# Decoder layer on one core: norm chains on VectorE at the start, unread products ahead of the first tokens, values a slot later, late turning

## The reference

```python
x = x + attn(layernorm(x))            # 32 heads of 32, 8 key/value heads, rotary, causal
x = x + xattn(layernorm(x), context)  # a matmul of two fake-quantised operands
x = x + ffn(layernorm(x))

def attn(x):
    q, k, v = split(x @ w_qkv.T + b_qkv)          # 1024, 256, 256 wide
    q, k = apply_rope(q), apply_rope(k)           # pairs (even, odd) turned by cos and sin
    scores = where(causal, q @ k.T / sqrt(32), -1e20)
    return softmax(scores) @ v @ w_o.T + b_o
def xattn(x1, x2):                                # x2: the context, 1024 x 1024
    fake_quant = lambda x, s, z: (clip(round(x / s + z), 0, 255) - z) * s
    return fake_quant(x1) @ fake_quant(x2)
def ffn(x):
    base = x @ W_org.T
    q = x.mean(axis=tokens) @ Wq.T                # one query of 128 per batch
    coeffs = softmax(q @ lora_keys.T / sqrt(128)) # 8 experts
    h = x @ lora_down                             # 8 experts of 64: 512 wide
    return base + (coeffs * h) @ lora_up
```

## Time and profile before

| | us |
|---|---|
| median of 3 runs | 791.65 |
| lowest, highest | 790.46, 792.01 |
| the profiled execution | 793.04 |
| its span (first to last instruction) | 791.2 |
| TensorE busy in it | 693.7 (88%) |
| TensorE's weight loads (beside its matmuls) | 556.9 (70%) |
| VectorE busy | 421.7 (53%) |
| ScalarE busy | 429.9 (54%) |
| GpSimd busy | 307.6 (39%) |

### The profile page before, as it was taken

One profiled execution on the slowest core, in us unless ns is written; L12 is line 12 of the kernel. 1 busy time (PEld: TensorE's weight loads), 2 busy tenths in 40 slices (PEclk: granted clock), 3 DMA queues, 4 the chain that ended last, 5 costly groups with the idle time before them and its releaser, 6 DMA issues.

```text
span 791.2 us, 12919 instructions
## 1 busy us (share of the span) xinstructions
PE 693.7 (88%) x4608; PEld 556.9 (70%) x4608; DVE 421.7 (53%) x1123; ACT 429.9 (54%) x1025; POOL 307.6 (39%) x384
## 2 busy tenths in 40 slices
PE   3999599999999899998768687799996787799998
PEld 3897477788777677875546475588875666588886
DVE  3366377776777536656648353433336569831212
ACT  3325378878787667797665653646314660512320
POOL 5337655543342534471304710505713011525510
PEclk9998899999999999999979698999999797699999
DMA  7504856563445606225350430403425342323102
GB/s 251 193 2 159 245 174 170 157 172 97 136 121 177 201 23 189 64 75 163 112 164 1 130 75 4 120 14 108 160 88 179 100 148 85 120 93 107 41 13 94
DMA packets 43823, 93.49 MB, mean 118 GB/s; under 512 B 5488, under 2 KB 5872, under 8 KB 42224
## 3 DMA queue, kind: packets, MB, share of 16 engines
q1 hardware_dynamic: 40176, 76.94, 30.2%
q0 software_dynamic: 3584, 15.73, 8.3%
HBM read 72.72 MB, written 19.92 MB: 117 GB/s over the span
## 4 chain that ended last, share of the span: by engine, by line
PE 58%; DVE 15%; POOL 9%; ACT 8%; issue 6%; DMA 2%; SPq 1%; DVEq 0%; ACTq 0%
PE dense L1023 37%; PE probt L917 7%; PE score L905 5%; PE pv L932 4%; POOL w_lo L1558 3%; PE score L1023 2%; DVE stats L1295 2%; DVE prob_all L1251 2%; ACT stage L1060 2%; ACT prob_all L1104 2%; POOL ln_s L828 2%; DVE act_t L1318 1%; POOL prob_all L1575 1%; POOL ln_s L830 1%; DVE prob_all L1344 1%
## 5 line engine op out<-in xcount | busy, mean ns | idle before, releaser
L1023 PE MATMUL dense<-w_hi,act_t 128*128 128x512 f32 (+1 forms) x684 | 233.4, 404 | 23.6 <-DVE act_t L1318 10.7
L1251 DVE CUSTOM_DVE_ANT_0 prob_all<-score,mask_sb 128x128 f32<-128x128 f32 (+3 forms) x256 | 123.7, 487 | 141.4 <-PE score L905 139.5
L1558 POOL TENSOR_TENSOR w_lo<-stage,w_hi 128x512 fp32r<-128x512 f32 x89 | 116.4, 1316 | 191.5 <-ACT w_hi L1064 191.2
L1104 ACT ACTIVATE prob_all<-prob_all,neg_max 128x128 f32<-128x128 f32 (+3 forms) x256 | 143.2, 559 | 72.4 <-DVE neg_max L1251 70.6
L1023 PEld LDWEIGHTS dense<-w_hi,act_t 128*128 128x128 f32 x684 | 133.3, 200 | 51.8 <-DVE act_t L1318 11.8
L1023 PE MATMUL dense<-w_lo,act_t 128*128 128x512 f32 (+1 forms) x372 | 138.5, 393 | 5.6 <-DVE xres L1389 3.1
L1023 PE MATMUL dense<-act_t,w_hi 128*128 128x512 f32 x408 | 139.6, 424 | 1.8 <-DVE xres L1367 1.8
L917 PE MATMUL probt<-ident_sb,prob_all 128*128 128x128 f32 x640 | 113.9, 277 | 1.4 <-ACT prob_all L1113 1.1
L905 PE MATMUL score<-k_stack,q_stack 96*128 96x128 f32 (+3 forms) x256 | 92.1, 364 | 13.9 <-DVE neg_max L1251 7.5
L1064 ACT ACTIVATE w_hi<-stage 128x512 fp32r<-128x512 f32 x117 | 71.9, 624 | 50.9 <-PE dense L1023 31.1
L1113 ACT ACTIVATE prob_all<-probt 128x128 f32<-128x128 f32 (+3 forms) x160 | 68.2, 426 | 47.0 <-PE probt L917 46.0
(11 more groups left out here) (156 smaller groups left out, 916.0 us busy)
## 6 DMA issues: line engine op xcount, KB each, us to landing
q_stack<-rope_dram POOLq DMA_DIRECT2D x16, 768.0 KB, 7.4
stage<-in_w_qk SPq DMA_DIRECT2D x40, 256.0 KB, 3.0
rope_dram<-act_t SPq DMA_DIRECT2D x40, 256.0 KB, 3.3
stage<-in_w_o SPq DMA_DIRECT2D x32, 256.0 KB, 3.0
stage<-in_ctx_kv SPq DMA_DIRECT2D x24, 256.0 KB, 3.1
stage<-in_w_org SPq DMA_DIRECT2D x24, 256.0 KB, 2.8
xres<-in_x SPq DMA_DIRECT2D x8, 512.0 KB, 6.6
prob_all<-in_x SPq DMA_DIRECT2D x8, 512.0 KB, 6.8
```

The lines of the kernel that those rows point to most:

```text
L1023: last = engine.matmul(dst, lhs, rhs, start=(k == 0 and c == 0), stop=(k == g.kts - 1 and c == len(pairs) - 1))
L1104: engine.activation(prob[:, u % P_SLOTS, 0:length], prob[:, u % P_SLOTS, 0:length], ACT.Exp, bias=neg_max[:, m:m + 1], scale=-1.0, accum_o ...
L1251: engine.tensor_tensor_reduce(prob[:, u % P_SLOTS, 0:length], score_bank[u % 2][:, 0:length], mask_sb[:, S - length:S], -1.0, HIGHEST, ALU ...
L1558: engine.tensor_tensor(slot_lo(p, 0, NW), raw_of(p), slot_hi(p, 0, NW).bitcast(F32), ALU.subtract).then_inc(g_piece, 1)
```

## The change

It has these parts:

- **Start.** The norm chains of norm (1, 0) run on VectorE. VectorE zeroes a 128x512 buffer (`blank`, the space of a query stack not yet in use), and TensorE runs sixteen 128x512 products on it into a bank of PSUM that nobody reads before its own first product overwrites it (`keep_clock`). The tokens of the next tile are turned in the middle of a tile's steps. SyncE fetches the last two x tiles behind the weight pieces, and ScalarE and VectorE have another order of their first steps to go with it.
- **Units.** The product with the values, and all that hangs on it, stands one unit later (`PV_LAG` 5; output products are ready one slot later too). A context piece is rounded one slot after its input was made, where the slot holds a unit. On VectorE the row maximum and the copies of turned probabilities stand ahead of the low parts of tokens. The odd pieces of the first base product of batch 0 have their low part on VectorE.
- **Behind the units.** A tile is turned only when its source lies 5.0 planned microseconds back instead of 1.2 (`LATE_TURN_US`), and quantising stands at the head of a slot on VectorE instead of its end.

The diff, cut to its core:

```diff
 PROBT_SLOTS = 6
+PV_LAG = 5
+BLANKS = 16
+LATE_TURN_US = 5.0
+TOKENS_LAG = 1
 MAX_SLOTS = 8
...
 TERMS = 3
-CHAINS_ON_VECTOR = ((2, 1), (3, 1))
+CHAINS_ON_VECTOR = ((1, 0), (2, 1), (3, 1))
 EARLY_LAGS = 2.0, 3.5, 4.5, 6.0, 9.5
...
             if cross:
-                self.note("round", j, p)
+                self.note("round", j + 1 if unit else j, p)
             else:
...
             return p % 2 == 0
-        return p < 8 and p % 2 == 1 or piece["kind"] == "q" and piece["b"] == 0 and piece["nb"] < 4 or piece["kind"] == "out" and p % 2 == 1
+        return p < 8 and p % 2 == 1 or piece["kind"] == "q" and piece["b"] == 0 and piece["nb"] < 4 or piece["kind"] == "out" and p % 2 == 1 or piece["kind"] == "base" and piece["b"] == 0 and piece["nb"] == 0 and p % 2 == 1
...
                 source = ("third", b, t) if which == 2 else ("apply", which, b, t)
-                if not self.past(j, source, 3 if unit else 1, now, 1.2):
+                if not self.past(j, source, 3 if unit else 1, now, 1.2 if unit else LATE_TURN_US):
                     continue
...
                     self.note("turn", j, (which, b, t, half))
-                    self.note("tokens", j + 1 if unit else j, (which, b, t, half))
+                    self.note("tokens", j + TOKENS_LAG if unit else j, (which, b, t, half))
                     halves.append(j)
...
             last = self.first_unit_slot + NT * GROUP * (NKV * g.b + k + 1) - 1
-            return j >= last + 9
+            return j >= last + PV_LAG + 5
         if g.kind == "cross":
...
         w_spaces += [(k_stack[:, 0, :], k_stack[:, 1, :])]
+        blank = q_stack[:, 0, 0, :]
         spare = values_sb[:, :, :, :].rearrange("p b t c -> p (b t c)")
...
         v_const = sem("v_const")
+        v_blank = sem("v_blank")
         v_round = sem("v_round")
...
             fetch(1)
+            fetch(2)
             load_x(0, 1)
-            fetch(2)
             fetch(3)
-            load_x(0, 2)
             engine.dma_start(bias_v[:, :], b_v.to_broadcast([P, VW])).then_inc(d_bv, 16)
...
             fetch(5)
-            load_x(0, 3)
             fetch(6)
             fetch(7)
+            load_x(0, 2)
+            load_x(0, 3)
             engine.dma_start(bias_qk[:, :], b_qk).then_inc(d_bqk, 16)
...
+            def keep_clock():
+                e.wait_ge(v_blank, 1)
+                for _ in range(BLANKS):
+                    engine.matmul(dense_bank[0][:, :], blank[:, 0:P], blank, start=True, stop=True)
...
                 u = j - first_unit
-                if j < NT:
+                if j == 0:
+                    keep_clock()
                     for half in range(2):
-                        turn_tokens(1, 0, j, half)
+                        turn_tokens(1, 0, 0, half)
                 for halves in at["turn"].get(j, ()):
...
                 for s in range(first, end):
+                    if j < NT - 1 and s == first + plan.token_steps // 2:
+                        for half in range(2):
+                            turn_tokens(1, 0, j + 1, half)
                     if plan.steps[s][0].kind == "down" and plan.steps[s][1:] == (0, WEIGH_AT):
...
                     step(s)
-                if 0 <= u - 4 < UNITS and (u - 4) % GROUP == GROUP - 1:
-                    values((u - 4) // GROUP)
-                for gi in ends_at(u, 4):
+                if 0 <= u - PV_LAG < UNITS and (u - PV_LAG) % GROUP == GROUP - 1:
+                    values((u - PV_LAG) // GROUP)
+                for gi in ends_at(u, PV_LAG):
                     turn_inverse(gi)
...
-            for made in range(4):
+            for made in range(2):
                 make_high(made)
             normalise(1, 0, 0)
+            make_high(2)
             for half in range(2):
                 tokens_high(1, 0, 0, half)
-            for made in range(4, 8):
+            make_high(3)
+            for made in (4, 5):
+                make_high(made)
+            normalise(1, 0, 1)
+            for made in (6, 7):
                 make_high(made)
...
                 if j < NT - 1:
-                    normalise(1, 0, j + 1)
+                    if j:
+                        normalise(1, 0, j + 1)
                     for half in range(2):
                         tokens_high(1, 0, j + 1, half)
-                for gi in ends_at(u, 5):
+                for gi in ends_at(u, PV_LAG + 1):
                     take_out_inverse(gi)
...
                     spread(gi)
-                for gi in ends_at(u, 7):
+                for gi in ends_at(u, PV_LAG + 3):
                     attn_high(gi)
...
+            engine.memset(blank[:, :].bitcast(F32), 0.0).then_inc(v_blank, 1)
             engine.memset(ones_r[:, :].bitcast(F32), 1.0).then_inc(v_const, 1)
-            for t in range(2):
-                for part in range(2):
-                    norm_stats(1, 0, t, part)
-            for made in (1, 3):
-                low_piece(made)
+            for part in range(2):
+                norm_stats(1, 0, 0, part)
+            low_piece(1)
             for half in range(2):
                 tokens_low(1, 0, 0, half)
+            low_piece(3)
+            for part in range(2):
+                norm_stats(1, 0, 1, part)
             for made in (5, 7):
...
                 u = j - first_unit
+                if j < NT - 1:
+                    for half in range(2):
+                        tokens_low(1, 0, j + 1, half)
                 if j < NT - 2:
...
                         norm_stats(1, 0, j + 2, part)
-                if j < NT - 1:
-                    for half in range(2):
-                        tokens_low(1, 0, j + 1, half)
                 if j == NT + 2:
...
                     constants()
+                if 0 <= u < UNITS:
+                    maximum(u)
+                if 0 <= u - 3 < UNITS and probt_on[u - 3] == "vector":
+                    take_out_turned(u - 3)
+                if not 0 <= u < UNITS:
+                    for b, t in at["second"].get(j, ()):
+                        quantise_second(b, t)
                 for which, b, t, half in at["tokens"].get(j, ()):
...
                         route_mean(b)
-                if 0 <= u < UNITS:
-                    maximum(u)
-                if 0 <= u - 3 < UNITS and probt_on[u - 3] == "vector":
-                    take_out_turned(u - 3)
                 for m, part in rotate_at.get(j, ()):
...
                     invert(gi)
-                for gi in ends_at(u, 6):
+                for gi in ends_at(u, PV_LAG + 2):
                     scale_values(gi)
...
                     norm_stats(*half)
-                for b, t in at["second"].get(j, ()):
-                    quantise_second(b, t)
+                if 0 <= u < UNITS:
+                    for b, t in at["second"].get(j, ()):
+                        quantise_second(b, t)
                 for b, t in at["third"].get(j - 1, ()):
...
                     load_stacks(gi)
-                for gi in ends_at(u, 7):
+                for gi in ends_at(u, PV_LAG + 3):
                     attn_low(gi)
...
                     add_output_bias(0, bias_at[j])
```

## The result

| | us |
|---|---|
| before, median of 4 (lowest, highest) | 791.83 (790.46, 793.52) |
| changed, median of 4 (lowest, highest) | 755.16 (754.24, 760.09) |
| changed / before | 0.9549, 95% interval 0.9502 to 0.9595 |
| the changed kernel in a second comparison (`again`) | 758.33, 0.9564 (0.9537 to 0.9591) |
| its profiled execution, span | 754.4, 752.6 |

The change made the kernel 34.5 to 35.7 us faster. The forecast was 768.0 with a range of 757 to 782: the direction was right, the size was a third too small.

A forecast was written before the change was run, and what follows sets the result against it. The prediction took TensorE's work plus four idle holes as the bound. Its gains, 8.9 + 1.5 + 6 + 7.5 = 23.9 us, taken from the profiled 793.04 gave 769.1, so 768 at the median, range 757 to 782.

The forecast's parts named there:

- start: Program start up to the first score: chains on VectorE and earlier tiles bring it 8.9 us earlier, bounds 4.2 and 11.1.
- values and out later: Units, 97 to 345: values and out products a slot later cut TensorE's waits, 1.5 us gain, bounds -1 and 3.5.
- rounding later: Units, 345 to 428: rounding a slot later removes VectorE's 23.0 us of waiting, 8 us gain, a third of it.
- odd base pieces on VectorE: Units: four low parts of the first base product move to VectorE beside its idle time, worth nothing.
- maximum first: Units, 428 to 543: tokens' low parts stand behind the row maximum eight times, 2 us loss.
- late turning: Behind the units: out steps ahead of the transposes fill their waits, 7.5 us gain, bounds 2 and 10.
- Rival 2: Units and tail: if the row maximum paces slots, the middle opens and the gain is 33.4, so 758; chance 0.2.
- The 3.2 us of the unread products: Program start: unread products raise the clock, so the first tile's transposes and 24 products save 3.2 us; bounds 0 and 3.2.
- Rival 3: Program start: the clock falls between unread products and transposes; the start loses 1 to 3 us, 771; chance 0.07.
- the collision that I allowed for: Program start: VectorE's chain and GpSimd's low parts share ports, 1.1 us per collision, one or two per chain.
- It is a move, priced 0: Units to behind the last unit: eight dense steps at 0.67 us, 5.3 us, only change place, at no cost.
- Rival 4: Units, 428 to 543: token parts behind the maximum make it slower, 796 at 3.5 us per group; chance 0.04.

The follow-up runs named there:

- before_round_later: Kernel before with context pieces rounded one slot after their input as the only change: 777.88 us, 0.9834.
- no_round_later: Changed kernel with context pieces rounded in the slot of their input again: 765.08 us, 0.9676.
- no_late_turning: Changed kernel with turning behind the units at 1.2 planned us and quantising at the end of VectorE's slot, as before: 763.37 us, 0.9653.
- gap_filled: Changed kernel with eight more unread 128x512 products between the first key products and the second tile's transposes: 753.78 us, 0.9529.
- no_unread_products: Changed kernel without the sixteen unread products: 754.45 us, 0.9529.
- start_and_late: Changed kernel without any of its edits in the units, so start and late turning only: 772.62 us, 0.9766.
- before_round_low: Kernel before with both the rounding a slot later and the odd low parts of the first base product on VectorE: 769.45 us, 0.9728.
- values_lag_4: Changed kernel with values and out products a slot earlier again (PV_LAG 4): 756.09 us, 0.9565.
- same_and_late_sum: Changed kernel with maximum behind tokens' low parts, no unread products, and context sum behind units 5.0 planned us after its last piece, not 0.6: 754.29 us, 0.9525.
- start_only: Changed kernel with its edits in the units and late turning undone, so only the start is left: 785.38 us, 0.9925.
- more_low_parts: Changed kernel with eight more unread products in the start's gap, maximum behind tokens' low parts, second base product's odd pieces also on VectorE: 755.81 us, 0.9544.

## Why the prediction was too small

By the steps of its sum, forecast against measured:

| step | forecast | measured |
|---|---|---|
| start | 8.9 | 5.9 alone |
| values and out later | 1.5 | 0 (by removal: 5.4 in the units, -5.1 behind them) |
| rounding later | 8 | 13.1 alone, 8.9 by removal |
| odd base pieces on VectorE | 0 | 6.4 alone, 5.1 by removal |
| maximum first | -2 | -3.9, -0.6 and -0.8 in three pairs |
| late turning | 7.5 | 12.6 with the start, 7.0 to 8.2 by removal |

The two halves measured on the kernel before (start with late turning 18.5, rounding with low parts 21.5) come to 40.0, the whole to 34.5 to 35.7; some 5 us are lost between them, little more than the noise of such a sum (3 to 4 us).

**The step that failed first** is "Odd base pieces move to VectorE, four low parts beside idle time: nothing". I looked at what the move costs VectorE and never at what it frees on GpSimd. In the waits of TensorE from 428 to 543, of which the earlier trace rows show one line, the line above it is the longer one:

```profile
PE dense L1023 <- POOL w_lo L1558: 7.6, 5, 3.5
```

And the chain of waits of the kernel before shows it between 432 and 456, in rows that I had not read:

```profile
432.50 0.26 POOL ln_s L833
432.77 1.73 POOL w_lo L1558
434.59 0.21 POOL ln_s L821
...
438.16 2.47 POOL w_lo L1558 x2
440.63 0.53 POOL k_stack L1535
...
445.38 1.23 POOL w_lo L1558
446.65 1.65 PE dense L1023 x3
...
451.35 1.27 POOL w_lo L1558
452.62 1.26 POOL act_t L1569
453.87 1.23 POOL w_lo L1558
455.15 0.97 PE dense L1023 x3
```

GpSimd has norm chains, six low parts (7.9 us) and the issue of two loads (`k_stack`, `q_stack`) one behind the other, and TensorE's base products hang on its last low part. Its busy share is small in the table (41.32 of 115), which is why I passed it over; but for some 20 us it was the engine in series. With the odd low parts on VectorE as the only change (`before_low_parts`) GpSimd's low parts are 4.5% of the chain of waits from 424 to 452, where they were 22.0% of it from 424 to 460, and the whole is 6.4 us faster. TensorE's own waits for them fall only from 7.6 to 6.2 us, and those for VectorE's low parts of tokens from 7.1 to 4.7. The step that failed is thus a cost put at nothing on the engine that the work left.

**The second** is "I take 8 us, a third of the VectorE wait": the rounding is worth 13.1 alone. The mechanism held: with this edit alone VectorE's waits for ScalarE's context input fall from 23.0 to 10.3 us, and TensorE's scores wait less for the maximum. Here are these waits of TensorE over all units, in the kernel before and in `before_round_later`:

```profile
PE score L905 <- DVE neg_max L1251: 7.5, 9, 1.7
```

```profile
PE score L905 <- DVE neg_max L1251: 2.8, 5, 1.1
```

That is 4.7 us; the rest of the gain isn't put down to one wait. The stretches from score 160 to 192, 192 to 224 and 224 to the last go from 73.6, 81.8 and 74.5 to 67.6, 71.6 and 69.7 us, with two steps fewer in each (1.3 us), and the mean granted clock in them from 0.98, 0.85 and 0.93 to 1.00, 0.90 and 1.00. The bound that I gave for rounding and maximum together, +13, held the rounding alone; to the sum I brought 8. Rival 2, the middle opens, was the nearer case (758 forecast). Its condition, that the row maximum paces the slots, is borne out only in part, by these 4.7 us.

**The start** came near the forecast at the first score of the first profiled execution (10.3 against 8.9), and that was luck of the execution: it was 4.0 in `again`, and the start alone gives 5.9. The 3.2 us of the unread products are not there. What is late next was in my own text ("TensorE is there at 15.9", "ready 17.8"); I counted this wait as 1.9 us and did not ask what the clock does in it. Rival 3 had the clock fall between the unread products and the transposes. That happened in two of the nine profiled executions (`no_round_later`, `no_late_turning`), in three more it fell in the first tile, and in these five tile 3 ended earliest; in the other four it fell behind the 1.8 us of waiting.

The rule on the shared ports (the Trainium skill, SBUF — State Buffer, "Who interferes with whom") is borne out in part. GpSimd's steps beside VectorE's low parts still stretch (0.66 for a step of 0.34), but VectorE's chain ran at its full pace, 2.58 us, though a low part of GpSimd (1.29 us) ran beside its first half: the collision that I allowed for didn't come. And transposes do run at the higher clock, 1.06 us for eight, as the row had it; by the Trainium skill (TensorE: Matmul & The Clock Gate, "Part 4: PE-mode transpose") they shouldn't. In the same place of the program eight of them took 1.06 us in `gap_filled` and 1.94 in `no_unread_products`. The measurement decides.

**Moved steps priced at nothing.** "It is a move, priced 0" is too cheap. With late turning, 324 steps behind the last unit take 245.4 us and 316 take 234.0 (the changed kernel and `start_and_late`); without it 254.5 and 245.2 (`no_late_turning` and the kernel before). Eight steps cost 11.4 and 9.3 us there, not 5.3. They are not alike: the six that move with the rounding cost 4.4 us on the kernel before (249.6 against 245.2), near the 4.0 of their price, and the two that move with the lag cost 5.1 more, with late turning (245.4 against 240.3) as without (254.5 against 249.4 in `before_round_low`). So what was priced wrong is the lag, whose out products also come a slot later. Part of the 11.4 is seen in the timeline of TensorE in the changed kernel, a wait for a low part of GpSimd:

```profile
522.13 0.74 PE L1035 MATMUL dense<-act_t,w_hi 128*128 128x512 f32 x2 [2.57 <-POOL w_lo L1586]
```

In the profiled execution of `values_lag_4` all waits for GpSimd's low parts behind the last score come to 0.9 us, in the changed kernel to 4.2. Why else the lag costs so much there isn't settled. It is why the lag is worth nothing though the units run faster with it. The 5 us lost between the halves stand in the same place: behind the last score they would give 11.2 - 4.2 = 7.0 us, and the changed kernel gives none (245.4 against 245.2).

**Late turning** held as a mechanism (the transposes' waits 14.0 with it undone, 1.7 with it), and 7.5 lies between its measurements. That it gives more where the eight steps aren't moved fits the paragraph above, but I have not shown how; taking the wait inside the context sum away gains nothing, as `same_and_late_sum` shows.

**The maximum** costs something between 0.6 and 3.9 us, and the 2 us that I gave it lie in the middle. The pair with 3.9 has the two-way start in it; the other two, 0.6 and 0.8, are each within the noise, and in the profiled executions all three have shorter units with the maximum behind the tokens (0.8 to 2.0, 3.0 and 4.3 us). Rival 4 didn't happen: TensorE waits 4.4 us for the tokens' low parts where it waited 7.1.

## What to carry to other kernels

An edit that hands work from one engine to another has two prices. Read the chain of waits, and the list of what TensorE waits for, for the engine that the work leaves, not only the idle time of the one that gets it; a low busy share says nothing about a stretch of 20 us in which that engine is in series.

Making an engine ready earlier makes it wait at the next thing, and for TensorE a wait can cost the clock of the work behind it: the 1.8 us before the second tile did so in all four profiled executions that had them. Fill the gap or leave the first part slow, but look at the executions one by one: a part with two outcomes 6 us apart stands in every comparison of its variants, and the same edit can come out at 3.9 us in one pair and at 0.6 in another.

A step that is moved behind the units has the price of its matmuls only if nothing else moves with it: six steps cost 4.4 us, two others 5.1.

## What the runs showed of the hardware

- Sixteen 128x512 products on zeros from a standing start took 5.26 to 6.77 us in twelve profiled executions. The distance from one product to the next is 0.43 us at first and 0.23 later, and the change comes at a different product each time, between the sixth and the fifteenth.
- After 1.8 us of standing still at 16 us, TensorE's granted clock was 0.52 to 0.65 over the next 8 us and 0.64 to 0.75 over the 9 behind them, in four executions of four (`again`, `start_only`, `start_and_late`, `values_lag_4`), and 1.00 throughout in the two (`gap_filled`, `more_low_parts`) where products on zeros filled those 1.8 us.
- Eight fp32 transposes of 128x128 on TensorE took 1.06 us at the higher clock and 1.94 at the lower in the same place (`gap_filled`, `no_unread_products`).
- A norm chain (statistics aggregated, then ten one-column steps) took 2.58 us on VectorE, its first half beside a low part of GpSimd, and 2.56 in the kernel before in the tail.
